# The two-term split beside a convolution: which of GpSimd and VectorE subtracts what, and when W is loaded

## What is computed

```python
K = 2 * einsum('hn,hnl->hl', Ct, exp(dtA * arange(512))).real    # 32 heads, 64 states
y = causal_convolution(x, K) + x * D[:, None]
x = x + y * (arange(512) < length[:, None])
A = lora_A_w[ids]; Bw = lora_B_w[ids]                            # 32 adapters of rank 16
x = x + (einsum('bsd,od->bso', x, base_weight) + base_bias
         + einsum('bsr,bor->bso', einsum('bsd,brd->bsr', x, A), Bw))
```

## Time and profile before

| | before |
|---|---|
| median of 3 runs (lowest to highest) | 217.97 us (217.53 to 218.04) |
| the profiled execution: time, span | 217.77 us, 215.8 us |
| busy: PE, PEld | 193.4 us (90%), 166.1 us (77%) |
| busy: DVE, ACT, POOL | 171.4 us (79%), 115.5 us (54%), 91.7 us (42%) |
| DMA | 56.45 MB, mean 262 GB/s |

### The profile page before, as it was taken

One profiled execution on the slowest core, in us unless ns is written; L12 is line 12 of the kernel. 1 busy time (PEld: TensorE's weight loads), 2 busy tenths in 40 slices (PEclk: granted clock), 3 DMA queues, 4 the chain that ended last, 5 costly groups with the idle time before them and its releaser, 6 DMA issues.

```text
span 215.8 us, 4336 instructions
## 1 busy us (share of the span) xinstructions
PE 193.4 (90%) x1050; PEld 166.1 (77%) x1050; DVE 171.4 (79%) x364; ACT 115.5 (54%) x330; POOL 91.7 (42%) x144
## 2 busy tenths in 40 slices
PE   0049999998989899989999999999999999999992
PEld 0046999897978789968888888888888888888881
DVE  3987898779799668588997888878787878878652
ACT  2737353543644442257667565666666575656530
POOL 4740000004355487077556444545545364545500
PEclk9999999999999999999999999999999999999999
DMA  5925999999999999957667676766667677765233
GB/s 134 298 99 156 385 403 407 408 413 407 406 412 408 405 412 386 401 177 206 207 218 252 198 219 193 237 194 222 205 203 235 194 222 200 232 187 182 101 106 133
DMA packets 21376, 56.45 MB, mean 262 GB/s; under 512 B 3378, under 2 KB 3826, under 8 KB 21106
## 3 DMA queue, kind: packets, MB, share of 16 engines
q1 hardware_dynamic: 18226, 47.78, 61.5%
...
q10 hardware_dynamic: 576, 0.13, 0.3%
...
## 4 chain that ended last, share of the span: by engine, by line
PE 72%; DMA 17%; DVE 5%; issue 1%; ACT 1%; POOL 1%; DVEq 0%
PE k_ps L921 21%; PE y_ps L921 21%; DMA strip<-k_pad 16%; PE z_ps L884 16%; PE z_ps L909 7%; PE y_ps L930 2%; PE y_ps L931 2%; PE k_ps L930 2%; PE k_ps L931 2%; DMA par<-params 1%; ACT mag L442 1%; PE y_ps L861 1%; DVE work L656 0%; DVE ex L598 0%; DVEq L89 0%
## 5 line engine op out<-in xcount | busy, mean ns | idle before, releaser
L884 PE MATMUL z_ps<-xp,strip 128*128 128x512 f32 (+3 forms) x384 | 65.0, 327 | 3.4 <-DMA strip<-k_pad 3.4
L884 PEld LDWEIGHTS z_ps<-xp,strip 128*128 128x128 f32 x384 | 59.8, 196 | 8.5 <-DMA strip<-k_pad 4.7
L411 POOL DMA_INDIRECT b_hl<-b_tab,b_idx x32 | 37.9, 1184 | 15.6 <-issue 9.9
L406 POOL CAST ag<-a_hl 128x128 fp32r x64 | 24.2, 381 | 43.3 <-PE z_ps L909 30.5
L921 PE MATMUL k_ps<-w_hi,xp 128*128 128x512 f32 x128 | 42.6, 393 | 0.0
L921 PE MATMUL y_ps<-w_hi,xp 128*128 128x512 f32 x128 | 42.5, 393 | 0.0
L519 ACT ACTIVATE ag<-a_hl 128x64 fp32r x128 | 25.7, 249 | 21.1 <-issue 21.0
L437 ACT ACTIVATE xp<-z_all 128x512 fp32r<-128x512 f32 x32 | 20.0, 628 | 28.2 <-PE z_ps L884 26.6
L713 DVE TENSOR_TENSOR xp<-z_all,xp 128x512 fp32r<-128x512 f32 x32 | 27.1, 849 | 4.7 <-ACT xp L437 4.5
L719 DVE TENSOR_TENSOR z_all<-z_ps,mask 128x512 f32<-128x512 f32 (+2 forms) x33 | 22.2, 672 | 7.5 <-PE z_ps L884 7.3
L921 PEld LDWEIGHTS k_ps<-w_hi,xp 128*128 128x128 f32 x128 | 24.0, 188 | 4.9
...
## 6 DMA issues: line engine op xcount, KB each, us to landing
strip<-k_pad SPq DMA_DIRECT2D x32, 512.0 KB, 10.4
z_all<-x_conv SPq DMA_DIRECT2D x16, 512.0 KB, 11.1
...
a_raw<-a_t SPq DMA_DIRECT2D x2, 512.0 KB, 11.1
x_t<-b_rows SPq DMA_DIRECT2D x2, 512.0 KB, 12.3
w_sb<-w_t SPq DMA_DIRECT2D x2, 512.0 KB, 12.5
b_tab<-b_hl SPq DMA_DIRECT2D x1, 1024.0 KB, 8.7
```

What stands on the lines that cost most here:

```text
L406: last = g.tensor_copy(ag[:, s, :, :, q, :].rearrange("p c e r -> p e c r"), src)
L411: g.indirect_dma_start(out=b_hl[:, t % BS, :].bitcast(F32), out_offset=None, in_=b_tab, in_offset=bass.IndirectOffsetOnAxis(ap=b_idx[:, t: ...
L884: last = nc.tensor.matmul(z_ps[:, h % ZS, m * P:L], strip[:, h % SS, m * P:(m + 1) * P, t], xp[:, h % XS, 0:LC - m, e, :], start=(n == 0), ...
```

## The change

1. **Who subtracts.** The 32 remainders of x go from DVE (`remainder(h)`) to a loop on POOL. The four remainders each of A, B's table and W go from POOL to DVE (`low_a`, `low_b` beside heads 15 to 25, `low_w` around tile 0's x).
2. **When W comes.** W's two halves are no longer loaded behind strips 22 and 24, but behind x tile 0, after the last strip. The unit matrix is added after POOL's first four gathers, W's high terms are made by ACT around tile 0's copy, its low terms by DVE; tile 0's base matmuls wait for W's chunks one by one.
3. **When x comes.** Seven pairs of heads instead of five are loaded at the start; the others, and A's first half, stand behind other strips.
4. **The start.** Two POOL subtractions/additions into `mm` stand before the wait for `th`; `th_1` is written as multiply and add; strip 0 is loaded in two halves, and head 0 waits for the second only before its third row of chunks; `keep_warm` issues 12 and 2 matmuls instead of 14 and 4.

```diff
-PRE = 5
-X_AT = {3: 5, 5: 6, 7: 7, 9: 8, 11: 9, 13: 10, 15: 11, 17: 12, 19: 13, 21: 14, 23: 15}
+PRE = 7
+X_AT = {5: 7, 7: 8, 10: 9, 13: 10, 15: 11, 17: 12, 19: 13, 21: 14, 23: 15}
 IDS_AT = 6
-A_AT, B_AT, W_AT = {8: 0, 12: 1}, {16: 0, 18: 1}, {22: 0, 24: 1}
+A_AT, B_AT = {9: 0, 12: 1}, {16: 0, 18: 1}
 SPLIT_A = {14: 0, 15: 1, 18: 2, 19: 3}
 SPLIT_B = {21: 0, 22: 1, 23: 2, 24: 3}
-SPLIT_W = {26: 0, 27: 1, 28: 2, 29: 3}
+LOW_A = {15: 0, 16: 1, 19: 2, 20: 3}
+LOW_B = {22: 0, 23: 1, 24: 2, 25: 3}
 K_AFTER = {2: 7, 3: 14}
-WARM_0, WARM_1 = 14, 4
+WARM_0, WARM_1 = 12, 2
 STEPS_AT = {2: (4, 5, 6, 7, 8, 9), 3: (11, 12, 13, 14, 15, 16)}
 QA = 2
 BC = AD * R // NW
@@ -184,7 +185,7 @@
         b_landed = [sem(f"b_landed{s}") for s in range(BS)]
...
-                src = bass.AP(tensor=k_pad.tensor, offset=k_pad.offset + 2 * (h * PAD + 1),
-                              ap=[[2, P], [1, 2 * L]])
-                sp.dma_start(strip[:, s, :, :].rearrange("p l e -> p (l e)").bitcast(F32), src).then_inc(strip_landed[s], 16)
+            def load_strip(h, s, j0, j1, done):
+
+                src = bass.AP(tensor=k_pad.tensor, offset=k_pad.offset + 2 * (h * PAD + 1 + j0),
+                              ap=[[2, P], [1, 2 * (j1 - j0)]])
+                sp.dma_start(strip[:, s, j0:j1, :].rearrange("p l e -> p (l e)").bitcast(F32), src).then_inc(done, 16)
...
+                if h == 0:
+                    load_strip(h, 0, 0, L // 2, strip_begun)
+                    load_strip(h, 0, L // 2, L, strip_landed[0])
+                else:
+                    load_strip(h, h % SS, 0, L, strip_landed[h % SS])
                 if h in X_AT:
                     load_pair(X_AT[h])
...
                     load_half(b_raw, b_rows, B_AT[h], b_in)
-                if h in W_AT:
-                    load_half(w_sb, w_t, W_AT[h], w_in)
...
                 sp.dma_start(x_t[:, s, :], x_tile[t]).then_inc(xt_landed[s], 16)
@@ -292,6 +295,8 @@
 
             sp.wait_ge(tab_lo, NW)
             load_x_tile(0, 0)
+            for n in range(2):
+                load_half(w_sb, w_t, n, w_in)
...
             store_table(0, b_hl[:, :, :].bitcast(F32), tab_hi_stored)
             store_table(1, b_lo, tab_lo_stored)
@@ -346,18 +351,18 @@
             link(g.tensor_tensor(sm[:, 4:6, :], par[:, 2:4, :], twice(ea[:, :]), ALU.mult))
             link(g.tensor_tensor(mm[:, 0, 0, :], sm[:, 4, :], sm[:, 6, :], ALU.subtract))
             link(g.tensor_tensor(mm[:, 0, 1, :], sm[:, 5, :], sm[:, 7, :], ALU.add))
+            link(g.tensor_tensor(mm[:, 1, 1, :], sm[:, 6, :], sm[:, 4, :], ALU.subtract))
+            link(g.tensor_tensor(mm[:, 1, 0, :], sm[:, 5, :], sm[:, 7, :], ALU.add))
             pool.wait_ge(th_ready, 1)
             g.tensor_scalar(rc[:, 1, :], th[:, :], -1.0, 1.0, ALU.mult, ALU.add).then_inc(rc_ready, 1)
...
-            link(g.tensor_scalar(th_1[:, :], th[:, :], 1.0, None, ALU.add))
+            link(g.tensor_scalar(th_1[:, :], th[:, :], 1.0, 1.0, ALU.mult, ALU.add))
             pool.wait_ge(turn_ready, 1)
             link(g.tensor_scalar(an[:, 0, :], turn, -0.25, None, ALU.is_lt))
             link(g.tensor_scalar(an[:, 0, :], an[:, 0, :], -0.25, None, ALU.add))
...
-            link(g.tensor_tensor(mm[:, 1, 1, :], sm[:, 6, :], sm[:, 4, :], ALU.subtract))
-            link(g.tensor_tensor(mm[:, 1, 0, :], sm[:, 5, :], sm[:, 7, :], ALU.add))
             four = mm[:, :, :, :].rearrange("p o t h -> p (o t) h")
...
             pool.wait_ge(own_ready, 1)
             link(g.memset(h_lo[BR:P, :, :].bitcast(F32), 0.0))
 
-            def split_w(n):
-
-                pool.wait_ge(w_hi_done, n + 1)
-                g.tensor_tensor(w_lo[:, n, :], w_sb[:, n, :], w_hi[:, n, :].bitcast(F32),
-                                ALU.subtract).then_inc(w_split, 1)
-
-            for n in range(NW):
-
-                part = slice(n * AD // NW, (n + 1) * AD // NW)
-                pool.wait_ge(a_hi_done, n + 1)
-                g.tensor_tensor(a_hl[:, part, 1, :], a_raw[:, part, :], a_hl[:, part, 0, :].bitcast(F32),
-                                ALU.subtract).then_inc(a_split, 1)
+            for h in range(NH):
+
+                pool.wait_ge(xc_hi_done, h + 1)
+                g.tensor_tensor(xp[:, h % XS, :, 1, :], z_all[:, h, :, :], xp[:, h % XS, :, 0, :].bitcast(F32),
+                                ALU.subtract).then_inc(xc_lo_done, 1)
...
             pool.wait_ge(a_split, NW)
-            for n in range(NW):
-
-                pool.wait_ge(tab_hi, n + 1)
-                g.tensor_tensor(b_lo[:, n, :], b_raw[:, n, :], b_hl[:, n, :].bitcast(F32),
-                                ALU.subtract).then_inc(tab_lo, 1)
-            for c in range(LC):
-                pool.wait_ge(w_in[c // 2], 16)
-                d = w_sb[:, c, c * P:(c + 1) * P]
-                g.tensor_tensor(d, d, eye[:, :], ALU.add).then_inc(w_eye, 1)
-            pool.wait_ge(w_eye, LC)
-            for n in range(LC):
-                split_w(n)
...
@@ -415,6 +401,10 @@
             pool.wait_ge(ids_ready, 1)
             for t in range(TS):
                 gather(t, t)
+            for c in range(LC):
+                pool.wait_ge(w_in[c // 2], 16)
+                d = w_sb[:, c, c * P:(c + 1) * P]
+                g.tensor_tensor(d, d, eye[:, :], ALU.add).then_inc(w_eye, 1)
...
-                if h in SPLIT_W:
-                    n = SPLIT_W[h]
-                    act.wait_ge(w_eye, n + 1)
-                    act.activation(w_hi[:, n, :], w_sb[:, n, :], ACT.Copy).then_inc(w_hi_done, 1)
+            def split_w(n):
+
+                act.wait_ge(w_eye, n + 1)
+                act.activation(w_hi[:, n, :], w_sb[:, n, :], ACT.Copy).then_inc(w_hi_done, 1)
...
+            gather(0, 0)
+            split_w(0)
+            split_w(1)
             act.wait_ge(x1_early, 1)
             act.activation(by_head(xp[:, 0, :, 0, :], 0, EARLY), by_head(in_chunks(x_t[:, 0, :]), 0, EARLY),
                            ACT.Copy).then_inc(xhi_early, 1)
-            gather(0, 0)
+            split_w(2)
+            split_w(3)
...
+            def low_a(n):
+
+                part = slice(n * AD // NW, (n + 1) * AD // NW)
+                dve.wait_ge(a_hi_done, n + 1)
+                V.tensor_tensor(a_hl[:, part, 1, :], a_raw[:, part, :], a_hl[:, part, 0, :].bitcast(F32),
+                                ALU.subtract).then_inc(a_split, 1)
+
+            def low_b(n):
+
+                dve.wait_ge(a_split, NW)
+                dve.wait_ge(tab_hi, n + 1)
+                V.tensor_tensor(b_lo[:, n, :], b_raw[:, n, :], b_hl[:, n, :].bitcast(F32),
+                                ALU.subtract).then_inc(tab_lo, 1)
+
+            def low_w(n):
+
+                dve.wait_ge(w_hi_done, n + 1)
+                V.tensor_tensor(w_lo[:, n, :], w_sb[:, n, :], w_hi[:, n, :].bitcast(F32),
+                                ALU.subtract).then_inc(w_split, 1)
...
             fraction()
             exponents_of(GROUPS[1][0], NH)
-            remainder(0)
-            remainder(1)
             multiply()
             scale()
             k_low(1)
-            remainder(2)
-            remainder(3)
...
@@ -752,7 +756,10 @@
                 for k, last in K_AFTER.items():
                     if h == last + XS:
                         k_low(k)
-                remainder(h)
+                if h in LOW_A:
+                    low_a(LOW_A[h])
+                if h in LOW_B:
+                    low_b(LOW_B[h])
                 if h in beside:
...
             part_of_x1(0, EARLY, x1_early)
+            low_w(0)
+            low_w(1)
             head(NH - 2)
...
             dve.wait_ge(xhi_done, 1)
             part_of_remainder(EARLY, NH, xlo_done)
+            low_w(2)
+            low_w(3)
...
+                if h == 0:
+                    pe.wait_ge(strip_begun, 16)
+                else:
+                    pe.wait_ge(strip_landed[h % SS], 16 * (h // SS + 1))
...
                 for n, (m, t, e) in enumerate(terms):
 
+                    if h == 0 and (m, t, e) == (LC // 2, 0, 0):
+                        pe.wait_ge(strip_landed[0], 16)
...
                 for n, (c, e, w) in enumerate(terms):
+                    if first and s == 0 and n % 3 == 0:
+                        pe.wait_ge(w_split, c + 1)
...
             tile_h(0, 0, True)
-            pe.wait_ge(w_split, NW)
             tile_base(0, 0, True)
```

More of the change, by code:

```diff
@@ L186, in build @@
         tab_hi_stored, tab_lo_stored = sem("tab_hi_stored"), sem("tab_lo_stored")
-        k_stored, pad_stored = sem("k_stored"), sem("pad_stored")
+        k_stored, pad_stored, strip_begun = sem("k_stored"), sem("pad_stored"), sem("strip_begun")
         pool_step, dve_step = sem("pool_step"), sem("dve_step")
@@ L249, in _ @@
                 load_pair(n)
-            def load_strip(h, s):
-                src = bass.AP(tensor=k_pad.tensor, offset=k_pad.offset + 2 * (h * PAD + 1),
-                              ap=[[2, P], [1, 2 * L]])
```

(19 more changed lines are left out.)

## The result

The change makes the kernel slower: 220.62 us (median of 7 runs, 218.09 to 221.94) against 217.97 (7 runs, 217.53 to 218.39), a ratio of 1.0094, 95% interval 1.0069 to 1.0118. The profiled execution took 221.94 us (span 220.2 us). It is the slowest of the seven and no part of the ratio, which goes by the other six (median 220.08 us), so what follows has every cost at its largest.

A forecast was written before the change was run, and what follows sets the result against it. Strip transfers were taken to bound the convolution, PE the tiles. The terms -5.0 (convolution), +2.5 (W's chain) and +1.0 (tile 1) sum to -1.5 us, taking 217.77 to 216.3 us; 8-in-10 range 213.0 to 218.4.

The forecast's parts named there:

- count of transfers: Strip loading: 512 KB units, numbered as SP asks for them from strip 0, land 1.293 us apart.
- 22.0 + 1.293 U: Strip loading before the change: time in us at which 512 KB unit number U lands.
- 0.5 us earlier origin: Start: the strips' queue begins 0.5 us earlier, so unit U lands at 21.5 + 1.293 U.
- Head 0 begins no earlier in my sum: Convolution's start: head 0 at 22.0 us, between 20.9 without a POOL and DVE collision in SBUF and 22.6 with two.
- the strips' bound: Convolution: strip transfers set its end at 86.6 us and cover smaller delays, whether head 0 begins at 20.9 or 22.0.
- the gain is eaten: Rival, chance 0.16: slow W additions, a collision or a clock fall before group 1 leave no gain; 217.8 to 218.1 us.
- may put group 3 back some 0.5 us: Convolution around head 16: POOL holding SBUF against DVE delays group 3 by some 0.5 us, covered by strip transfers.
- -5.0 for the convolution: Convolution's end: fewer transfers ahead of the strips move it from 91.6 to 86.6 us, a gain of 5.0.
- +2.5 for W's chain: Between convolution and tile 0: POOL's gathers and additions, then W's copies and low terms, delay `tile_h` by 2.5 us.
- +1.0 for `low_w(2)` and `low_w(3)`: Ahead of tile 1: these two DVE steps stand before its x and cost PE 1.0 us.
- W is not late: Rival at tile 0, chance 0.26: faster POOL gathers shrink the 2.5 us to 0.3 or less; 214.1 us.
- POOL sets the pace: Rival in the convolution, chance 0.11: POOL's step exceeds PE's 1.96 us a head; 220.3 us at 2.1 a head.

The follow-up runs named there:

- e9_steps: e7_wearly with 16 warm matmuls behind group 0 instead of 12 and group 3's DVE steps one head earlier; 214.77 us.
- e10_wlater: e9_steps with W's halves loaded behind strips 25 and 26 instead of 22 and 24, its splits beside heads 29 to 31; 213.85 us.
- e8_best: e2_first4 with bias loaded before B's stores, 16 warm matmuls instead of 12, six more before tile 0, group 3's steps one head earlier; 215.27 us.
- e2_first4: The changed kernel with the x remainders of heads 0 to 3 back on DVE; 216.30 us.
- e5_hold: The changed kernel with POOL waiting for group 1's factors before its x remainders, all 32 still on POOL; 217.20 us.
- e1_warm: The changed kernel with 26 warm matmuls behind group 0 instead of 12; 218.86 us.
- e4_noswap: e2_first4 with all x remainders on DVE and those of A and B back on POOL, W still late; 215.97 us.
- e11_xdve: e7_wearly with all x remainders on DVE and those of A and B back on POOL; 215.01 us.
- e12_cold: The kernel before the change with 2 warm matmuls behind group 0 instead of 14; 217.92 us.
- e7_wearly: e2_first4 with W loaded behind strips 22 and 24 again, its terms made beside heads 27 to 31 and just after; 214.94 us.

## Why the prediction was wrong

**The bound and the count of transfers: right.** In e9_steps and e10_wlater strips land by 22.0 + 1.293 U: head 25 as unit 41 at 75.07 (formula 75.0), head 27 as unit 43 at 77.19 (77.6). The 0.5 us earlier origin did not come in most traces: e8_best's head 20 waited for unit 32 until 63.46, which is 22.0 + 41.4. Only e10_wlater has some 0.4 us of it (head 20 at 63.05, head 27 at 77.19).

**The step that failed first: "Head 0 begins no earlier in my sum ... I take 22.0", and that the strips' bound covers the rest.** I had the lock, its price of 1.29 us and its place, and took 22.0, with 22.6 for two waits. The rows show three waits, of which the first was hidden behind ACT; the other two cost 1.7 us, so that head 0 would have begun near 23.0 at the full clock, by e2_first4's 21.17 and 21.6 instead of 19.85 for the factors. It began at 23.84, the rest being low clock in group 1 and the two warm matmuls (0.9 us). What failed is that this is covered: "it is the transfers that set the size, whether head 0 begins at 20.9 or 22.0". By my own formula a head 0 at 23.84 puts head 20 at 64.4, behind its strip's 62.9, and from there PE sets the convolution's end. The trace has PE waiting for no strip at all, where I had named head 20's. e2_first4 and e5_hold take the collision away and have group 1's factors back before 20 us; that is shown.

**The clock was mis-sized as a rival.** It was a part of "the gain is eaten" (0.16), for one place. It fell at three. PE idles before group 1 because that is late (2.92 us), before group 3, and before tile 0, and 3 to 7 us at 1.2 GHz go with each. One cause feeds the next: the fall cost 1.7 us in the first heads, and with head 0 late no strip is waited for any more, so every further microsecond of PE counts. e1_warm gives the first fall 1.4 to 1.8 us of time by itself. By the seven executions all low clock together is an estimated 2.0 us (218.09 to the 216.1 drawn out) to 5.8 us (221.94). The forecast of 216.3 is about what is left without it.

**Group 3: "may put group 3 back some 0.5 us; the strips' bound covers that".** Put at 0.5, it was 1.75 us. The reason I gave, POOL in DVE's way, is at most a part: without any remainder of x on POOL it is 1.32 (e4_noswap) and 1.23 (e11_xdve). DVE makes group 3's steps one by one beside the heads. Before, waits for strips held PE back at heads 10, 13 and 14 until group 3 was there; a PE that is not held back meets it early. Two runs bear this out: e12_cold, the kernel before with a PE that no longer waits visibly for these strips, shows 1.20 us, and with the steps one head earlier the wait is gone (e8_best, e9_steps). That the strips' bound covers it is right where that bound stands: e7_wearly with 1.71 us of it and e9_steps without differ by 0.17 us.

**The handover: -5.0 for the convolution, +2.5 for W's chain, +1.0 for `low_w(2)` and `low_w(3)`.** In e2_first4, where the start is mended, the convolution ends at 87.5 us (said: 86.6), tile 0 stands 1.74 us behind it (said: 3.6), and tile 1 5.17 behind that (said: 4.55). W's chain cost 0.7 instead of 2.5: POOL's four gathers were through 2.7 us behind its last remainder (81.77 to 84.48), where I gave them 4.3. That is the rival "W is not late", which I had put at 0.26. Tile 1 cost 1.6 instead of 1.0, part of it low clock (a tile 0 at 0.93 us for `tile_h`), and DVE's wait of 1.12 us for the bias I had not seen. I had counted B's tables behind W, and not the bias behind them. That the sum's 216.3 is what e2_first4 measures (216.30) is luck: its terms err against each other.

**The rival "POOL sets the pace" did not happen,** though the time lies in its band (above 218.6). POOL's 32 remainders took 1.39 us each, inside 1.96, and POOL waited 27.4 us for ACT's copies between them; the kernel is slower by another road.

**W late, by the terms of the sum, gives 2.6 us of transfers and costs 3.5 us behind them.** The sum hid this loss of 0.9 us in one gain of 5.0, of which the early pairs are the other half. Between e2_first4 and e7_wearly the loss is 1.4 us of median, part of it clock; between e8_best and e9_steps, with the clock up in both, it is 0.5. e10_wlater shows that a place in between is best.
